# One residual step fewer on node rows: edge rows, a dense first round and a scattered output in a four-layer graph kernel

## The chip, the cores and the metric
One core of one Trainium2 chip runs the whole kernel. The metric is device microseconds of an execution, as the median of the runs shown. One more execution was taken with the hardware profiler; all rows of the trace come from it.

## What is computed
The graph has N = 50000 nodes of width D = 96 and 50000 edges `src -> dst`, sorted by `dst`. Four layers follow each other, each as x = x + layer(relu(layernorm(x))):

```python
x = x + gnn0(h)      # attention with K, Q, V and an edge term, summed per destination
x = x + gnn1(h)      # gated messages from x[src] and 32 edge features, summed, then an MLP and a layernorm
# gnn2: 16 rounds of smoothing over the graph with self loops
h = h0
for _ in range(16):
    h = 0.9 * segment_sum(norm * h[row], col) + 0.1 * h0
x = x + h
# gnn3: one weighted graph convolution with self loops, norm = dinv[row] * ew * dinv[col]
h = relu(layernorm(x))
x = x + segment_sum((h @ W)[row] * norm, col) + b
```

A node that no edge points to has only its self loop: its smoothed value stays its start value, and its last layer needs no neighbour.

## The kernel before
**Layout.** Rows are padded to 128 partitions x 392 columns (`CH`), and one batch is J = 8 columns of all partitions, 1024 rows of 96 floats (384 KB). A pass over nodes or edges has `NB` = 49 batches. Because the edges are sorted by destination, a segment sum is a running sum down the columns of a partition: `scan_step` (L344) issues 16 small VectorE instructions for a batch, and a 128x128 product with `B` carries sums over partition borders at the end of a pass. The sum of a segment stands in the row of the segment's last edge. Segments that begin in an earlier partition are finished in 128 auxiliary rows.

**Gathers.** Whatever a row needs from another row is fetched by `gathers` (L337): eight indirect DMAs for a batch, issued by GpSimd (POOL), each for 128 rows. Stores and plain loads are issued by SyncE (SP).

**Stages.** They run one after the other. Each is a block with its own semaphores, and `retire` (L202) clears these between two stages. I name a stage by the prefix of its tiles:
- n0 (L514): layernorm and the K, V, Q product on nodes; scatters the pointer of each segment into `info_t`.
- e0 (L683): attention on edges, two gathers for a batch (16 issues).
- n1 (L818), e1 (L904): nodes, then edges, of the second layer, one gather for a batch each.
- n2 (L1057): the MLP of the second layer, x2, and the start value y0 of the smoothing, stored to x2_t and to both y tables (L1098).
- r1 (L1255): the first of 16 rounds. From here on the state of a node with in-edges lives in the row of its segment's last edge (tile `H`), so a round is one gather and one scan on edge rows. r1 fetches both y[src] and the start value y[dst], 16 issues for a batch, and stores c_t.
- r (L1354): 15 more rounds in one loop, 8 issues for a batch. A round's first gather waits until all rows of the round before are stored (L1395).
- n3 (L1476): back on node rows: gathers the last round's value, forms x3, layernorm, the product with W, and stores x3_t and z_t.
- e3 (L1594): gathers z[src], weighs and sums it on edge rows, stores agg3_t.
- n4 (L1657): gathers agg3 for each node, forms the output, stores it densely.

**Order.** `skewed` (L111) writes each engine's program as ticks: in tick t each stage function of the engine is run for batch t minus its lag, in the order of the list. K = 4 buffers stand between POOL and the compute engines in the skewed stages; r1, e3, n4 and e0 use two (`batches`, L132, and `ahead`, L143).

Of the kernel before, what the change touches and what calls it, by code (L numbers as in the profile page):

```python
# [17 lines left out]
P = 128  # L18
N = 50000
# [19 lines left out]
VALUES = ROWS  # L39
ROUNDS = 16  # L40
ALPHA = 0.1
NONE = 65535
WZ = D + HEADS
# [67 lines left out]
def skewed(eng, *stages):  # L111


    def tick(q, u):
        for lag, run in stages:
            n, h = q + (u - lag) // K, (u - lag) % K
            if not isinstance(q, int) or 0 <= K * n + h < NB:
                run(K * n + h, n, h)
# [3 lines left out]
    last = (NB - 1 + min(min(lags), 0)) // K  # L122
# [5 lines left out]
    for t in range(last * K, NB + max(lags)):  # L128
        tick(t // K, t % K)
# [28 lines left out]
def program(nc, x, src, dst, edge_attr_32, edge_attr_96, edge_weight,  # L158
# [13 lines left out]
    agg3_t = dram("agg3_t", REG + 1, D)  # L172
# [12 lines left out]
    with outer:  # L185
# [42 lines left out]

        def load_padded(eng, tile, whole, tail, b, done):
# [21 lines left out]
        k_e = sb("k_e", [P, CH])  # L251
        k_z = sb("k_z", [P, 1])
        ptr_n = sb("ptr_n", [P, CH])
        ptr_i = sb("ptr_i", [P, CH], I32)
        yptr_i = sb("yptr_i", [P, CH], I32)
        root = sb("root", [P, CH])
        iroot = sb("iroot", [P, CH])
        dinv = sb("dinv", [P, CH])
# [40 lines left out]
        r_all = sb("r_all", [P, 3, D])  # L299

# [60 lines left out]
        def pointers(own, ptr, no, start, t, to, base):  # L361

            own.do(V.scalar_tensor_tensor(out=t, in0=ptr[:], scalar=-1.0, in1=start[:], op0=ALU.mult, op1=ALU.add))
            own.do(V.tensor_scalar(t, t, -float(base), None, ALU.add))
            own.do(V.tensor_tensor(t, t, no[:], ALU.mult))
            own.do(V.scalar_tensor_tensor(out=t, in0=ptr[:], scalar=float(base), in1=t, op0=ALU.add, op1=ALU.add))
            own.add(V.tensor_copy(to[:], t))


        with ExitStack() as ph:  # L370
# [12 lines left out]
            aux_f = sb("aux_f", [P, 1], F32, ph)  # L383
            tmp = sb("tmp", [P, CH], F32, ph)
# [16 lines left out]
            with nc.Block() as block:  # L401
                @block.sync
                def _(sp):
# [13 lines left out]
                    for t in (agg0_t, agg1_t, agg3_t):  # L417
# [3 lines left out]
                    sp.wait_ge(s_tail, 16 * 12)  # L421
# [4 lines left out]
                def _(pool):  # L426
# [10 lines left out]
                    G.iota(aux_i[:], [[1, 1]], base=AUX, channel_multiplier=1).then_inc(s_iota, 1)  # L437
# [1306 lines left out]
```

## Time and profile before

| | us |
|---|---|
| median of 3 runs | 15979.43 |
| range of the runs | 15961.53 to 15987.55 |
| span of the profiled execution, first to last instruction | 13552.9 |
| time outside the span (median less span) | 2426.5 |
| POOL busy | 9980.6, 74% |
| DVE (VectorE) busy | 6176.6, 46% |
| PE (TensorE) busy | 6161.5, 45% |
| ACT (ScalarE) busy | 3099.7, 23% |

The profiled execution's own time is given as its span alone; what lies around it is known only as the difference to the median. Busy time counts instructions, not the time between the issues of two DMAs. Because the stages follow each other, an average over the span says little: a stage is read by itself, from its first to its last POOL instruction.

### The profile page before, as it was taken

How to read it: one execution, taken by the hardware profiler on the slowest of the kernel's cores; microseconds unless marked ns; L12 is line 12 of the kernel's file. 1: busy time of each engine (PE TensorE's matmuls, PEld its weight loads, DVE VectorE, ACT ScalarE, POOL GpSimd, SP SyncE). 2: the span in 40 equal slices, each digit the busy share in tenths (PEclk: the TensorE clock that was granted, in tenths of full speed). 3: DMA queues.
4: the chain of work that ended last, by engine and by line, in shares of the span. 5: the costliest groups of instructions: out<-in, count | busy, mean ns of one | idle time of the engine just before them, and what ended most of it. 6: DMA issues, size and time to landing. Idle time of an engine off the chain costs nothing. (4 is left out here: it accounts for less than half of the span.)

```text
span 13552.9 us, 124135 instructions
## 1 busy us (share of the span) xinstructions
PE 6161.5 (45%) x16702; PEld 3564.8 (26%) x16702; DVE 6176.6 (46%) x21955; ACT 3099.7 (23%) x11470; POOL 9980.6 (74%) x10210
## 2 busy tenths in 40 slices
PE   6422105873002555555555555555555555544000
PEld 4322103542001322223323332323322322233000
DVE  4344455596343444444444444444444444444533
ACT  5300133394000222222222222222222222233000
POOL 7677777676777777777777777777777777777777
PEclk8655557886555777777777777777777777755555
DMA  5433353374223333333333333333333333344245
GB/s 150 120 99 100 109 145 97 92 216 142 76 75 89 117 112 112 118 112 112 116 112 112 118 112 112 116 112 112 117 112 112 116 113 112 116 132 129 73 116 140
DMA packets 855833, 1558.86 MB, mean 115 GB/s; under 512 B 321698, under 2 KB 378674, under 8 KB 855666
## 3 DMA queue, kind: packets, MB, share of 16 engines
q1 hardware_dynamic: 523217, 1053.28, 22.9%
q0 software_dynamic: 332448, 504.04, 16.3%
q14 instruction: 148, 1.20, 0.0%
q8 instruction: 20, 0.33, 0.0%
HBM read 954.90 MB, written 602.08 MB: 115 GB/s over the span
## 5 line engine op out<-in xcount | busy, mean ns | idle before, releaser
L340 POOL DMA_INDIRECT r_g<-y_t,idx_s x6272 | 6051.0, 965 | 2128.7 <-issue 2115.0
L349 DVE SCALAR_TENSOR_TENSOR r_S<-r_S,scan_s,r_g 128x96 f32<-128x96 f32 x6272 | 2020.3, 322 | 4670.1 <-DMA r_g<-y_t,idx_s 3968.8
L1421 PE MATMUL r_pu<-r_S,ident 128*128 128x384 f32 x2940 | 1883.7, 787 | 3127.9 <-DVE F L351 3127.9
L1443 ACT ACTIVATE H<-r_pu,k_e 128x96 f32 (+1 forms) x5880 | 1443.3, 356 | 6059.3 <-PE r_pu L1421 6059.3
L351 DVE SCALAR_TENSOR_TENSOR F<-r_g,scan_s,F 128x96 f32<-128x96 f32 x6272 | 1967.6, 314 | 0.0
L1421 PEld LDWEIGHTS r_pu<-r_S,ident 128*128 128x128 f32 x2940 | 737.9, 276 | 3947.0 <-DVE F L351 3583.5
L1415 PE MATMUL r_pu<-H,ident 128*128 (+1 forms) x2940 | 1633.0, 646 | 101.5 <-DMA r_c<-c_t 101.5
L340 POOL DMA_INDIRECT n_ag<-agg_t,idx_s x1176 | 1227.2, 1044 | 395.8 <-issue 368.4
L1416 PE MATMUL r_pu<-r_c,ident 128*128 128x384 f32 x2940 | 1441.4, 578 | 0.0
L1415 PEld LDWEIGHTS r_pu<-H,ident 128*128 128x128 f32 x2940 | 824.4, 281 | 816.9 <-issue 683.4
L1416 PEld LDWEIGHTS r_pu<-r_c,ident 128*128 128x128 f32 x2940 | 712.4, 242 | 599.2 <-issue 383.0
L340 POOL DMA_INDIRECT e_g<-z_t,idx_s x392 | 397.2, 1013 | 148.5 <-issue 120.8
L340 POOL DMA_INDIRECT n_y<-y_t,idx_s x392 | 403.0, 1028 | 135.4 <-issue 118.0
L751 PE MATMUL e_eo<-w_e,e_eaT 97*128 97x96 f32 x784 | 182.7, 428 | 676.3 <-ACT e_eaT L772 676.3
L1297 PE MATMUL r_pc<-r_S,B 128*128 128x96 f32 x2 | 0.7, 475 | 1059.9 <-DVE H L1342 1059.9
L556 POOL DMA_INDIRECT info_t<-seg_s,idx_s x392 | 382.1, 975 | 120.2 <-issue 119.2
L1289 POOL DMA_INDIRECT r_c<-y_t,r_dst_s x392 | 378.0, 964 | 119.5 <-issue 119.5
L340 POOL DMA_INDIRECT e_kv<-kv_t,idx_s x392 | 377.9, 964 | 119.4 <-issue 119.4
L340 POOL DMA_INDIRECT e_x<-rec_t,idx_s x392 | 375.4, 958 | 119.4 <-issue 117.0
L731 POOL DMA_INDIRECT e_q<-q_t,dst_s x392 | 371.2, 947 | 119.5 <-issue 114.3
L349 DVE SCALAR_TENSOR_TENSOR e_S<-e_S,scan_s,e_g 128x96 f32<-128x96 f32 (+1 forms) x1176 | 380.3, 323 | 58.0 <-DVE e_g L800 9.4
L351 DVE SCALAR_TENSOR_TENSOR F<-e_g,scan_s,F 128x96 f32<-128x96 f32 (+1 forms) x1176 | 375.6, 319 | 0.0
(233 smaller groups left out, 7251.4 us busy)
## 6 DMA issues: line engine op xcount, KB each, us to landing
y_t<-H SPq DMA_DIRECT2D x784, 384.0 KB, 2.4
r_c<-c_t SPq DMA_DIRECT2D x735, 384.0 KB
r_g<-y_t,idx_s POOLq DMA_INDIRECT x6272
n_x<-x_t SPq DMA_DIRECT2D x147, 384.0 KB, 4.5
kv_t<-n_kvq SPq DMA_DIRECT2D x49, 768.0 KB, 3.7
agg_t<-e_S SPq DMA_DIRECT2D x98, 384.0 KB, 2.6
x_t<-n_x SPq DMA_DIRECT2D x98, 384.0 KB, 2.4
y_t<-n_y SPq DMA_DIRECT2D x98, 384.0 KB
```

The lines of the kernel that those rows point to most:

```text
L340: G.indirect_dma_start(out=to(j), out_offset=None, in_=table, in_offset=bass.IndirectOffsetOnAxis(ap=idx_s[:, h, j:j + 1], axis=0)).then_i ...
L349: own.add(V.scalar_tensor_tensor(out=S[:, h % slots, j, 0:w], in0=before, scalar=scan_s[:, h, j, 0:1], in1=g[:, j, 0:w], op0=ALU.mult, op1 ...
L351: last = V.scalar_tensor_tensor(out=F[:, 0:w], in0=g[:, j, 0:w], scalar=scan_s[:, h, j, 1:2], in1=F[:, 0:w], op0=ALU.mult, op1=ALU.add)
L556: G.indirect_dma_start(out=info_t, out_offset=bass.IndirectOffsetOnAxis(ap=idx_s[:, h, j:j + 1], axis=0), in_=seg_s[:, h, j, :], in_offset ...
L731: G.indirect_dma_start(out=gq[:, h, j, :], out_offset=None, in_=q_t, in_offset=bass.IndirectOffsetOnAxis(ap=dst_s[:, h, j:j + 1], axis=0)) ...
L751: last = T.matmul(eo[g][:, j, :], eaT[:, h, g, j * P:(j + 1) * P], w_e[:], start=True, stop=True)
L1289: G.indirect_dma_start(out=cs[:, h, j, :], out_offset=None, in_=y_t[0][0:ROWS, :], in_offset=bass.IndirectOffsetOnAxis(ap=dst_s[:, h, j:j ...
L1297: T.matmul(pc[:], B[:], S[:, 0, J - 1, :], start=True, stop=True).then_inc(s_cr, 1)
L1415: T.matmul(pu[h % 2][g][:], ident[:], cols(H, b)[:, c, :], start=True, stop=False)
L1416: T.matmul(pu[h % 2][g][:], ident[:], cs[:, h % 2, c, :], start=False, stop=False)
L1421: last = T.matmul(pu[h % 2][g][:], ident[:], S[:, h % 2, 4 * g:4 * g + 4, :], start=False, stop=True)
L1443: last = A.activation(v[:, j, :], pu[h % 2][j // 4][:, j % 4, :], ACT.Copy, scale=k[:, j:j + 1])
```

## The change
- n2 stores one wide table `yx_t` (start value, x2 and five degree factors, 197 floats a row) in place of x2_t. The two y tables are now stored out of the first 96 columns of that tile. ScalarE copies the degree factors into it.
- r1 becomes r0. Its second gather fetches the 788-byte rows of yx_t by `dst` where it fetched 384-byte rows of y; it keeps the degree factors per edge row and stores x2 per edge row too. In the same stage all nodes are treated as if they had no in-edges: dense load of yx_t, x3, layernorm, product with W, output, stores to z_t and to `out`.
- The loop r has 14 rounds where it had 15 (`MID`).
- A new stage l does the last round: after the scan it forms x3, layernorm and the product with W on edge rows, and stores both there. It takes the place of n3.
- e3 gathers z, sums, and finishes the output on edge rows (four more VectorE operations for a batch), and scatters it into `out` with eight indirect DMAs for a batch. Rows that end no segment are skipped by an index out of bounds. n4 and agg3_t are gone.
- In l and e3 a 50th batch (`NX`) handles the auxiliary rows; the tables on edge rows have eight more columns (`CHS`). The pointer arithmetic for y rows is replaced by a pointer that n0 scatters along.

```diff
-VALUES = ROWS
+CHS = CH + J
+SLOTS = P * CHS
+YW = 2 * D + 5
+NX = NB + 1
+OFX = [len(range(h, NX, K)) for h in range(K)]
...
-    x2_t = dram("x2_t", ROWS, D)
-    x3_t = dram("x3_t", ROWS, D)
+    yx_t = dram("yx_t", ROWS, YW)
+    x2s_t = dram("x2s_t", SLOTS, D)
+    x3s_t = dram("x3s_t", SLOTS, D)
     rec_t = dram("rec_t", ROWS, TR)
-    y_t = [dram(f"y{k}_t", VALUES + REG, D) for k in range(2)]
-    c_t = dram("c_t", ROWS, D)
-    z_t = dram("z_t", ROWS, D)
+    y_t = [dram(f"y{k}_t", ROWS + SLOTS, D) for k in range(2)]
+    c_t = dram("c_t", SLOTS, D)
+    z_t = dram("z_t", ROWS + SLOTS, D)
...
-                        after(sp, s_x2, b + 1)
-                        sp.dma_start(rows_of(x2_t, 0, b), x2[:, h]).then_inc(s_st[h], 16)
+                        after(sp, s_kc, b + 1)
                         after(sp, s_y0, b + 1)
+                        sp.dma_start(rows_of(yx_t, 0, b), yx[:, h]).then_inc(s_st[h], 16)
                         for t in y_t:
-                            sp.dma_start(rows_of(t, 0, b), y0[:, h]).then_inc(s_st[h], 16)
+                            sp.dma_start(rows_of(t, 0, b), yx[:, h, :, 0:D]).then_inc(s_st[h], 16)
...
+                        A.copy(yx[:, h, :, 2 * D:YW], cols(kc_n, b)).then_inc(s_kc, 1)
+                        ln_norm(act, b, yx[:, h, :, D:2 * D], yx[:, h, :, 0:D], rn2[:, h], s_sn, ACT.Relu
+                                ).then_inc(s_y0, 1)
...
+                    skewed(sp, (-5, load), (0, store_z), (1, store_c), (2, store_y))
...
+                    def step(b, n, h):
+                        after(pool, s_ix, 2 * b + 2)
+                        after(pool, s_y, b - 3)
+                        pool.wait_ge(s_cx[h], 32 * n)
                         gathers(y_t[0][0:ROWS, :], lambda j: g_[:, h, j, :], h, s_g[h])
                         for j in range(J):
+                            G.indirect_dma_start(out=yx[:, h, j, :], out_offset=None, in_=yx_t,
                                                  in_offset=bass.IndirectOffsetOnAxis(ap=dst_s[:, h, j:j + 1], axis=0)
...
+                    skewed(pe, (0, product), (-1, turn))
...
+                    skewed(act, (-2, slots), (1, keep), (-2, norm), (-1, turned),
+                           (-3, lambda b, n, h: ln_root(act, b, mv[:, h], rn[:, h], s_mv, s_sd)))
...
+                    def begin(b, n, h):
+                        after(dve, s_kc, b + 1)
+                        dve.wait_ge(s_cx[h], 32 * n)
+                        V.tensor_tensor(cs[:, h], yx[:, h, :, 0:D], wide(kc_e, b, 1), ALU.mult).then_inc(s_ck, 1)
+                        after(dve, s_ck, b + 1)
+                        ownb.step(b)
+                        ownb.add(V.tensor_tensor(bt[:, h % 2], cs[:, h], yx[:, h, :, 0:D], ALU.add))
+                        ownb.end()
+                    def value(b, n, h):
+                        own.step(b)
+                        after(dve, s_ms, b + 1)
...
+                        dve.wait_ge(s_st[h], 16 * n)
+                        after(dve, s_b, b + 1)
+                        own.do(V.tensor_tensor(ys[:, h], S[:, h % 2], bt[:, h % 2], ALU.add))
+                        V.tensor_tensor(ys[:, h], ys[:, h], wide(kc_e, b, 0), ALU.mult).then_inc(s_y, 1)
+                    def add(b, n, h):
+                        dve.wait_ge(s_xn[h], 16 * (n + 1))
+                        after(dve, s_h, b - 3)
+                        V.tensor_tensor(x3[:, h], xn[:, h % 2, :, 0:D], xn[:, h % 2, :, D:2 * D], ALU.add
+                                        ).then_inc(s_x3, 1)
+                        after(dve, s_x3, b + 1)
+                        after(dve, s_rn, b - 3)
+                        ln_stats(dve, own1, b, x3[:, h], st[:, h], mv[:, h], s_mv)
...
+                    def finish(b, n, h):
+                        dve.wait_ge(s_sz[h], 16 * n)
+                        for g in range(2):
+                            c = slice(4 * g, 4 * g + 4)
+                            after(dve, s_pz, 2 * b + 1 + g)
+                            V.tensor_copy(zt[:, h, c, :], po[g][:]).then_inc(s_z, 1)
+                        after(dve, s_z, 2 * b + 2)
+                        dve.wait_ge(s_so[h], 48 * n)
+                        own3.step(b)
+                        own3.do(V.tensor_tensor(ot[:, h], zt[:, h], x3[:, h], ALU.add))
+                        own3.end()
+                        V.tensor_tensor(ot[:, h], ot[:, h], r_all[:, 2:3, :].to_broadcast([P, J, D]), ALU.add
+                                        ).then_inc(s_o, 1)
+                    skewed(dve, (-2, scale), (0, finish), (-3, add), (1, begin), (1, value))
+                    finish_round(dve, first, s_cr, 1, zx[:, 0:D], s_zv, pc)
...
+            MID = ROUNDS - 2
...
+                    skewed(sp, (-1, edges_only(load)), (0, edges_only(load_x2)), (2, store_x3), (5, store_z), total=NX)
...
-                        gathers(y_t[1], lambda j: yg[:, h, j, :], h, s_g[h])
+                        after(pool, s_ss, b - 3)
+                        gathers(y_t[0], lambda j: g_[:, h, j, :], h, s_g[h])
                     skewed(pool, (0, step))
...
+                    skewed(pe, (1, edges_only(add)), (0, edges_only(start)), (5, product), (4, turn), total=NX)
...
+                    def value(b, n, h):
+                        after(act, s_up, b + 1)
+                        after(act, s_x3, b - 1)
+                        for j in range(J):
+                            last = A.activation(xv[:, h % 2, j, :], pu[h % 2][j // 4][:, j % 4, :], ACT.Copy,
+                                                scale=cols(kc_e, b)[:, j, 4:5])
+                        last.then_inc(s_xv, 1)
+                    def weigh(b, n, h):
+                        act.wait_ge(s_sz[h], 16 * n)
+                        for j in range(J):
+                            if j % 4 == 0:
+                                after(act, s_pz, 2 * b + 1 + j // 4)
+                            last = A.activation(zt[:, h, j, :], po[j // 4][:, j % 4, :], ACT.Copy,
+                                                scale=cols(kc_e, b)[:, j, 3:4])
+                        last.then_inc(s_z, 1)
+                    skewed(act, (-2, edges_only(slots)), (1, edges_only(value)), (3, norm), (5, weigh), (4, turned),
+                           (2, lambda b, n, h: ln_root(act, b, mv[:, h], rn[:, h], s_mv, s_sd)), total=NX)
...
+                    def sums(b, n, h):
+                        own.step(b)
+                        after(dve, s_ms, b + 1)
+                        after(dve, s_up, b - 1)
+                        s_g.wait(dve, h, 16 * J * (n + 1))
+                        scan_step(dve, own, h, D, g_[:, h], S, 2, s_ss, b + 1)
+                        own.end()
...
+                    skewed(dve, (0, edges_only(sums)), (3, scale), (2, add), total=NX)
...
+                    def scatter(b, n, h):
+                        after(pool, s_io, b + 1)
+                        after(pool, s_o, b + 1)
+                        pool.sem_inc(s_turn_p)
+                        for j in range(1 if isinstance(b, int) and b == NB else J):
+                            G.indirect_dma_start(
+                                out=out, out_offset=bass.IndirectOffsetOnAxis(ap=dst_s[:, h, j:j + 1], axis=0),
+                                in_=ot[:, h, j, :], in_offset=None, bounds_check=bound, oob_is_err=False
+                            ).then_inc(s_d[h], 16)
+                    skewed(pool, (0, edges_only(step)), (2, scatter), total=NX)
+                    for h in range(K):
...
+                            own.do(V.tensor_tensor(g_[:, h], g_[:, h], scan_s[:, h, :, 2:3].to_broadcast([P, J, D]),
+                                                   ALU.mult))
+                            scan_step(dve, own, h, D, g_[:, h], S)
+                            s_d.wait(dve, h, 16 * J * n)
+                            dve.wait_ge(s_ld[h], 32 * (n + 1))
+                            own.do(V.tensor_tensor(ot[:, h], S[:, h % 2], zo[:, h], ALU.add))
+                            c, w = slice(0, J), J
+                        v = ot[:, h, c, :]
+                        own.do(V.tensor_tensor(v, v, cols(kc_e, b)[:, c, 3:4].to_broadcast([P, w, D]), ALU.mult))
+                        own.do(V.tensor_tensor(v, v, x3[:, h, c, :], ALU.add))
+                        V.tensor_tensor(v, v, r_all[:, 2:3, :].to_broadcast([P, w, D]), ALU.add).then_inc(s_o, 1)
+                        if not end:
+                            own.end()
...
-                        gathers(agg3_t, lambda j: ag[:, h, j, :], h, s_g[h])
```

## Rows read from the trace of the kernel before

**Rows 1.** The page: span, and busy time by engine.
```profile
span 13552.9 us, 124135 instructions
PE 6161.5 (45%) x16702; PEld 3564.8 (26%) x16702; DVE 6176.6 (46%) x21955; ACT 3099.7 (23%) x11470; POOL 9980.6 (74%) x10210
```
**Rows 2.** Groups by line, POOL: count | busy us, mean ns | idle before.
```profile
L340 POOL DMA_INDIRECT r_g<-y_t,idx_s x6272 | 6051.0, 965 | 2128.7 <-issue 2115.0 <-ACT scan_s L1437 12.1 <-DVE F L351 1.5
...
L556 POOL DMA_INDIRECT info_t<-seg_s,idx_s x392 | 382.1, 975 | 120.2 <-issue 119.2 <-DVE seg_s L571 1.0
...
L340 POOL DMA_INDIRECT e_kv<-kv_t,idx_s x392 | 377.9, 964 | 119.4 <-issue 119.4
```
**Rows 3.** Timeline of POOL at stage borders: start us, us, instruction [idle before].
```profile
3178.75 0.95 POOL L340 DMA_INDIRECT n_ag<-agg_t,idx_s  x1 [0.31 <-issue]
3233.36 0.95 POOL L1280 DMA_INDIRECT r_zc<-y_t,idx_z  x1 [53.66 <-ACT scan_s L1309]
...
4270.12 0.95 POOL L340 DMA_INDIRECT r_g<-y_t,idx_s  x1 [12.13 <-ACT scan_s L1437]
...
4778.77 0.95 POOL L340 DMA_INDIRECT r_g<-y_t,idx_s  x1 [14.03 <-issue]
...
11927.68 0.95 POOL L340 DMA_INDIRECT n_y<-y_t,idx_s  x1 [16.15 <-ACT idx_s L1557]
...
12473.98 0.95 POOL L340 DMA_INDIRECT e_g<-z_t,idx_s  x1 [24.12 <-ACT scan_s L1631]
...
13008.18 0.95 POOL L340 DMA_INDIRECT n_ag<-agg_t,idx_s  x1 [12.58 <-issue]
...
13541.67 0.95 POOL L340 DMA_INDIRECT n_ag<-agg_t,idx_s  x1 [0.30 <-issue]
```
**Rows 4.** Timeline of DVE and POOL inside one batch of r1.
```profile
3257.38 0.96 DVE L1338 TENSOR_TENSOR r_c<-r_c,r_t 128x768 f32<-128x768 f32 x1
3257.57 1.58 POOL L340 DMA_INDIRECT r_g<-y_t,idx_s  x1 [0.30 <-issue]
...
3706.57 0.34 DVE L349 SCALAR_TENSOR_TENSOR r_S<-r_S,scan_s,r_g 128x96 f32<-128x96 f32 x1 [6.47 <-DMA r_g<-y_t,idx_s]
...
3710.92 0.31 DVE L351 SCALAR_TENSOR_TENSOR F<-r_g,scan_s,F 128x96 f32<-128x96 f32 x1
```
**Rows 5.** Timeline of ACT and DVE: one batch of r, one of n3.
```profile
8002.77 0.27 ACT L1437 COPY scan_s<-scan 128x24 f32 x1
...
8012.36 1.96 ACT L1443 ACTIVATE H<-r_pu,k_e 128x96 f32 x8 [9.31 <-PE r_pu L1421]
...
12208.45 1.38 DVE L306 BATCH_NORM_STATS2 n_st<-n_x 128x6 f32<-128x96 f32 x8
...
12209.98 0.64 DVE L311 BATCH_NORM_AGGREGATE n_mv<-n_st 128x2 f32<-128x6 f32 x8 [0.15 <-DVE n_st L306]
...
12211.50 1.02 DVE L1548 TENSOR_TENSOR n_z<-n_po,dinv 128x384 f32<-128x384 f32 x2
12211.55 2.97 ACT L329 ACTIVATE n_h<-n_x,n_rn 128x96 f32<-128x96 f32 x8 [0.51 <-DVE n_rn L322]
...
12214.43 1.04 ACT L1567 COPY n_hT<-n_tp 96x512 f32<-96x512 f32 x2
```
**Rows 6.** Windows of r, n3, n2 (ten batches): us, busy by engine, PEclk, DMA share, GB/s.
```profile
4275.00:11920.00 7645.00, 4423.50 (x8845) 2282.72 (x8844) 3264.34 (x11816) 1586.53 (x7334) 5640.60 (x5876) 0.78 0.38 113
11920.00:12470.00 550.00, 265.56 (x1180) 241.23 (x1178) 262.20 (x1082) 214.47 (x596) 402.96 (x392) 0.52 0.44 141
...
2886.00:2992.00 106.00, 84.48 (x398) 51.63 (x397) 99.07 (x455) 100.65 (x226) 81.91 (x80) 0.89 0.76 222
```
**Rows 7.** SP's DMA queue in n0 (60 to 520) and n2 (2690 to 3170): packets, MB, share.
```profile
q1 hardware_dynamic: 103530, 71.61, 49.9%
...
q1 hardware_dynamic: 30757, 84.21, 51.0%
```

More of the change, by code:

```diff
@@ L127, in skewed @@
             tick(q, u)
-    for t in range(last * K, NB + max(lags)):
+    for t in range(last * K, total + max(lags)):
         tick(t // K, t % K)
@@ new lines, in program, with wide, first_slots, finish_round @@
+        nodes.close()
+        def wide(t, b, k):
+            return cols(t, b)[:, :, k:k + 1].to_broadcast([P, J, D])
+        def first_slots(table, first):
+            return table[first:first + SLOTS, :].rearrange("(p j) d -> p j d", p=P)[:, CH, :]
+        def finish_round(dve, own, s_cr, count, before, s_z, pc):
+            dve.wait_ge(s_cr, count)
+            own.do(V.tensor_tensor(Z[:, 0:D], F[:, 0:D], pc[:], ALU.add))
+            own.add(V.memset(F[:], 0.0))
+            own.do(V.tensor_tensor(Z[:, 0:D], Z[:, 0:D], before, ALU.add))
+            V.scalar_tensor_tensor(out=zs[:], in0=Z[:, 0:D], scalar=zx[:, 2 * D:2 * D + 1], in1=z0[:], op0=ALU.mult,
+                                   op1=ALU.add).then_inc(s_z, 1)
@@ new lines, in product @@
+                    def product(b, n, h):
+                        for g in range(2):
+                            after(pe, s_tc, 2 * b + 1 + g)
+                            after(pe, s_z, 2 * b - 1 + g)
+                            for j in range(4):
+                                last = T.matmul(po[g][:, j, :], hT[:, h % 2, g, j * P:(j + 1) * P], w_3[:],
+                                                start=True, stop=True)
+                            last.then_inc(s_pz, 1)
+                    skewed(pe, (0, product), (-1, turn))
@@ L1310, in _, with keep @@
-                    batches(act, step)
+                        A.copy(idx_s[:, h, :], cols(src_i, b)).then_inc(s_ix, 1)
+                        s_d.wait(act, h, 16 * J * n)
+                        A.copy(dst_s[:, h, :], cols(dst_i, b)).then_inc(s_ix, 1)
+                        after(act, s_y, b - 3)
+                        A.copy(scan_s[:, h], cols(scan, b)).then_inc(s_ms, 1)
+                    def keep(b, n, h):
+                        s_d.wait(act, h, 16 * J * (n + 1))
+                        A.copy(cols(kc_e, b), yx[:, h, :, 2 * D:YW]).then_inc(s_kc, 1)
@@ L1626, in _, with slots @@
                 @block.scalar
                 def _(act):
-                    def step(n, h):
-                        act.wait_ge(s_s[h], n)
-                        gather_slots(act, n, h, src_i, s_ix, s_g, 16 * J)
-                        A.copy(scan_s[:, h], cols(scan, 2 * n + h)).then_inc(s_ix[h], 1)
-                    batches(act, step)
+                    def slots(b, n, h):
+                        s_g.wait(act, h, 16 * J * n)
+                        A.copy(idx_s[:, h, :], cols(row_e, b)).then_inc(s_ix, 1)
+                        after(act, s_o, b - 3)
+                        A.copy(scan_s[:, h], cols(scan, b)).then_inc(s_ms, 1)
@@ L1634, in _, with out_slots @@
+                    def out_slots(b, n, h):
+                        s_d.wait(act, h, 16 * J * n)
+                        A.copy(dst_s[:, h, :], cols(out_e, b)).then_inc(s_io, 1)
+                    skewed(act, (-2, edges_only(slots)), (1, out_slots), total=NX)
                 @block.vector
                 def _(dve):
-                    own = Own(dve, s_own, 1 + 2 * J - 1)
-                    own.add(V.memset(S[:], 0.0))
-                    own.do(V.memset(F[:], 0.0))
-                    own.loop()
```

653 lines of the change are left out of this document (341 added, 312 removed).

## The prediction, made before the changed kernel ran

> **What bounds the kernel now.** I read the page first: POOL is busy 74% of the span, no other engine half of it [rows 1]. Then the groups by line for POOL: an indirect DMA holds POOL for 0.95 to 0.98 us whether it gathers 384-byte rows, 768-byte rows (e_kv) or scatters (info_t), and 0.30 us passes before the next [rows 2]. So one issue costs 1.25 us when nothing disturbs it, whatever the row size. The code has 26 passes of 392 issues and one more: 10193, and 10193 x 1.25 = 12741 us of the 13552.9 us span. The kernel is a queue of issues; the other 812 us are idle stage borders and lengthened issues. The timeline of POOL at the borders gives each stage its own length (a stage ends where the next starts, less the idle time shown) [rows 3]:
> - r1: 3234.6 to 4258.0, 1023.4 us, 20.89 for a batch of 16 issues (quiet: 20.0).
> - r: 4270.1 to 11911.5, 7641.4 us, 509.4 for a round including 14.0 between rounds; inside a round 10.11 for a batch of 8 (quiet: 10.0).
> - n3: 522.2, 10.66 a batch. e3: 521.6, 10.65. n4: 534.4, 10.91, and 10.3 us after its last issue.
> - Borders: 53.7 (into r1), 12.1, 16.2, 24.1, 12.6.
>
> What lengthens an issue is seen inside r1 [rows 4]: POOL's instruction that starts at 3257.57, within a VectorE operation on 768 elements with two SBUF inputs, takes 1.58 us where 0.95 is usual. Only an issue that starts inside such an operation pays, so the excess per batch is small: 0.11 us with the scan alone (r), 0.65 with the scan and one wide operation (e3), 0.66 with two (n3), 0.89 with the scan and four (r1), 0.91 with four (n4).
>
> **The change, in issues.** Removed: one round, n3, n4 and r1's sixteen, that is 392 x 5. Added: r0's sixteen, l's eight, the scatter's eight in e3, 392 x 4, and one for the auxiliary rows. Left are 9802, 391 fewer: 489 us at 1.25. The rest is what the new stages give back.
>
> **n2.** Its work is changed in three places. (a) ScalarE copies 40 numbers a partition for each batch, 0.2 to 0.3 us (24 numbers take 0.27 [rows 5]). ACT is busy 100.65 of 106 us for ten batches of 10.6 [rows 6], so 0.53 us a batch is free and covers it; without that cover it would be 10 to 15 us. (b) The wide store adds 101 floats to 1024 rows, 414 KB; SP's queue moves 84.21 MB in 51.0% of 480 us on 16 engines, 21.5 bytes per ns and engine [rows 7], so 1.2 us a batch. (c) The two y stores go out in pieces of 384 bytes. n0 does that with q_t, next to other stores, and runs at 19.5 [rows 7]; if q_t alone makes the difference, a 384 KB store costs 0.45 us more, two of them 0.9. The DMA share of 0.76 [rows 6] is 8.1 us of 10.6; with 1.2 and 0.9 it is 10.2, just under the pace. Bounds: nothing, or 1 us a batch (49 us) if a nearly full queue holds the gathers back. I take 15, near nothing, since 10.2 is still below 10.6.
>
> The Trainium skill, "DMA: Bandwidth & Descriptors", section Specifications, says that transfers below 512 bytes make the DMA engine read, modify and write. If that doubled the y stores, n2 would be DMA-bound at 11.6 us and the time 34 us above my forecast. The rate of n0 shows a far smaller surcharge.
>
> **r0 for r1.** 16 issues, 20.0 us quiet; the longer rows change nothing for POOL, as e_kv shows [rows 2]. VectorE now has per batch: the scan 4.7 us [rows 4], seven wide operations of 0.96 (begin 2, value 2, add 1, finish 2), statistics 2.0, two copies out of PSUM about 1.0 [rows 5], 0.4 of scale: 15 us of 20. ACT has norm 2.97, the transposed copies 1.04 and some copies, about 5. Both fit. The dense part runs two to five ticks ahead through its lags and waits for nothing that POOL produces, and POOL waits for value of four batches back, 60 us of cover. SP issues eight transfers a batch where r1 has two, and waits inside them for s_z, s_o, s_ck, s_y in turn; behind it stands only the load five batches ahead. So the stage stays paced by issues. Excess: not below r1's 0.89, since scan and four operations are still there; n3's 0.66 stands for the dense part; together with one more operation up to 1.75, and 2.9 if each of three separate runs of wide operations catches an issue (3 x 0.65 + 0.9). I take 2.0: 22.0 x 49 = 1078. Its first gather comes later than r1's: ACT's list puts the root of batch 0 ahead of the first index copy, so it waits for a load, an add and statistics: about 10 us more. The border behind it grows from 12.1 to 22, since the scan and begin (6.7 us) now stand behind the last landing, and a copy of out_tail.
>
> **Rounds.** 14 x 509.4 = 7132. The first round also loads H, 384 KB a batch beside 38% DMA share [rows 6]: nothing. Border 16.
>
> **l for n3.** Eight issues, POOL waits for sums of four batches back. VectorE: 4.7 + 1.0 + 2.0 + 0.4 = 8.1. ACT: value 1.96, weigh the same, norm 2.97, copies 1.04 [rows 5], root and slots 0.8: 8.7. PE does what it does in r (4423.5 / 735 = 6.0) and in n3 (265.6 / 49 = 5.4) [rows 6]: 11.4 at the clocks of those windows, 0.78 and 0.52. In n2, where PE has 8.4 us of work in 10.6, the clock is 0.89; scaled to it the sum is 5.3 + 3.2 = 8.5. I take POOL's pace with e3's excess, 10.65 x 49 = 522; bounds 10.1 (r's) and 11.4. The border behind l: n2's 53.7 had a lag of six ticks, n3's 24.1 one of four; l has five and one batch more: 42.
>
> **e3 with the output for e3 and n4.** The same issues as the two together, and their wide operations: 10.65 + 10.91 = 21.56 x 49 = 1056; VectorE has 9.5 us of work in it. The scatter waits for a batch finished a whole tick earlier, so the gather of the next batch is never held up. One issue and the tail: 11.6.
>
> **Sum** from r1's first gather to the end: before 10318. After 10 + 1078 + 22 + 7132 + 16 + 522 + 42 + 1056 + 12 = 9890, 428 less; with n2's 15, 413 less. The span goes to 13140. Outside the span lie 2426 us that no row explains; neither stages nor loops can be seen in it, so I carry it over: 15979 - 413 = about 15565. Were it in proportion to the span (x 1.179), the gain would be 487 and the time 15490.
>
> **Rivals.**
> - *Another engine paces a stage.* In l PE at n3's clock: 6.0 x 0.78 / 0.52 + 5.4 = 14.4 us a batch, 184 us more; with n2 at its upper bound 49 - 15 = 34 more: about 15785. For it: PE waits for other engines in every tick, and n3's low clock. Against it: in n2 the same kind of load has 0.89.
> - *VectorE shuts POOL out, slower than before.* If an issue could not run during any VectorE operation with two SBUF inputs, r0 would take 20.0 + 6.7 + 5.0 = 31.7 (475 us over my term), e3 20.0 + 4.8 + 5.0 = 29.8 (404), l 16.0 (262): 16706. It decides from 39% of that, where the 413 and a further 32 are used up. Against it: r1 would need 28.8 and takes 20.89. For it: r0 leaves VectorE only 5 us free, more crowded than any stage shown. The Trainium skill, "SBUF — State Buffer", section "SBUF: two separate sides", calls the port pair of VectorE and GpSimd an exclusive lock taken also by operations with two SBUF inputs; the trace agrees that such a stall exists, and disagrees that it costs the operation's whole time.
> - *The saving is larger.* r0 at 0.89, e3 at one scan's 0.65, l at 10.1, no surcharge in n2: 140 us less, with the proportional outside 15979 - 553 x 1.179, about 15330.
> - *The change doesn't do what it says,* because idle borders or a serial first stage eat the 489 us: about 15980.
>
> **How the numbers follow.** Forecast 80%; another engine 10%; larger saving 5%; lock-out 3%; nothing 2%. The terms' bounds are, below: r0 -54, e3 -45, l -26, n2 -15, borders -28; above: r0 +43, l +37, n2 +34, borders +12. Half of the proportional outside's 74 goes below. That gives 15400 to 15700, which leaves out most of the 10% above and 5% below. A measurement tells about 0.2%, 32 us, from no change. Faster 0.93 (the first three, less some), same 0.02, slower 0.05.
>
> **What would show it.** POOL's issues: 9802. r0 near 22.0 us a batch and l near 10.7, with POOL idle before issues at 0.30; a wait of POOL on s_y or s_ss would prove another pace. e3 near 21.6. n2 still 10.6 a batch with DMA share near 0.95. Borders of 64, 22, 16, 42 us. Wrong would be a stage whose POOL idle time grows, a mean issue above 1.15 us in r0, or a time outside the span that moved.

## The result, and the profile after

On the chip of the first comparison the changed kernel took 15560.61 us (median of 4 runs, 15546.08 to 15589.12) and the kernel before 15983.49 (median of 4, 15961.53 to 16002.94): a ratio of 0.9737, 95% interval 0.9723 to 0.9751, or 423 us less. The forecast was 15565.

The page of the changed kernel's profiled execution, to be read beside [rows 1], and POOL's groups by line, beside [rows 2] (count | busy us, mean ns | idle before, with what ended it):

```profile
span 15555.2 us, 127954 instructions
PE 6190.4 (40%) x17902; PEld 3704.8 (24%) x17902; DVE 6357.5 (41%) x22965; ACT 3386.6 (22%) x12470; POOL 9532.1 (61%) x9820
```

```profile
L352 POOL DMA_INDIRECT r_g<-y_t,idx_s x5880 | 5634.2, 958 | 3590.5 <-issue 1924.0 <-ACT scan_s L1575 1452.6 <-DVE r_y L1443 177.9
...
L1830 POOL DMA_INDIRECT out<-e_o,e_out_s x393 | 417.7, 1063 | 174.8 <-issue 174.5 <-DVE e_o L1885 0.3
L1353 POOL DMA_INDIRECT r_yx<-yx_t,r_dst_s x392 | 402.0, 1025 | 119.4 <-issue 118.5 <-DVE r_y L1443 0.6 <-DMA x2s_t<-r_yx 0.3
```

POOL does what was forecast: 449 us less busy than in [rows 1], the same mean issue, a scatter of output rows at 1063 ns and a gather of 788-byte rows at 1025. But the span is 2000 us longer than that of the kernel before, and this execution took 15557.04 us, only 1.8 us more than its span. The 2426 us that the prediction carried "outside the span" are inside it. They are gaps, and they repeat. POOL at the borders of r and inside a round (start, us, instruction [idle before <- what ended it]):

```profile
5207.78 0.94 POOL L352 DMA_INDIRECT r_g<-y_t,idx_s  x1 [22.59 <-ACT scan_s L1575]
...
8016.19 0.94 POOL L352 DMA_INDIRECT r_g<-y_t,idx_s  x1 [6.10 <-ACT scan_s L1575]
...
8052.86 0.99 POOL L352 DMA_INDIRECT r_g<-y_t,idx_s  x1 [6.88 <-ACT scan_s L1575]
...
13723.83 0.94 POOL L352 DMA_INDIRECT l_g<-y_t,idx_s  x1 [22.36 <-ACT idx_s L1721]
```

Between the two middle rows lie 24 issues (29.8 us) and one gap, 36.7 us in all, and so it goes on through all rounds. A round takes 607 us here ((13723.83 - 22.36 - 5207.78) / 14) where [rows 3] gave 509.4. Whether the kernel, the change or the chip makes these gaps can't be told from this profile: it was the first question for the experiments.

### The profile page after: what moved, and what is told of

It reads as the page before. It is cut to its first block and busy times, and to the rows that moved or that the text cites. A ratio compares the mean times of both kernels' runs of the same rounds, so it can differ in the third digit from the quotient of the medians.

```text
span 15555.2 us, 127954 instructions
## 1 busy us (share of the span) xinstructions
PE 6190.4 (40%) x17902; PEld 3704.8 (24%) x17902; DVE 6357.5 (41%) x22965; ACT 3386.6 (22%) x12470; POOL 9532.1 (61%) x9820
## 5 line engine op out<-in xcount | busy, mean ns | idle before, releaser
L352 POOL DMA_INDIRECT r_g<-y_t,idx_s x5880 | 5634.2, 958 | 3590.5 <-issue 1924.0
L361 DVE SCALAR_TENSOR_TENSOR r_S<-r_S,scan_s,r_g 128x96 f32<-128x96 f32 x5880 | 1884.9, 321 | 5521.0 <-remote 3601.6
L1581 ACT ACTIVATE H<-r_pu,kc_e 128x96 f32 (+1 forms) x5488 | 1350.5, 368 | 7020.0 <-remote 4524.4
L1559 PE MATMUL r_pu<-r_S,ident 128*128 128x384 f32 x2744 | 1111.1, 531 | 650.6 <-remote 265.9
L352 POOL DMA_INDIRECT n_ag<-agg_t,idx_s x784 | 780.4, 995 | 457.3 <-issue 236.8
L1559 PEld LDWEIGHTS r_pu<-r_S,ident 128*128 128x128 f32 x2744 | 586.5, 217 | 1133.1 <-issue 374.3
L352 POOL DMA_INDIRECT l_g<-y_t,idx_s x392 | 386.4, 986 | 288.5 <-ACT idx_s L1721 120.4
L1373 PE MATMUL d_po<-w,d_hT 96*128 96x96 f32 x784 | 186.7, 430 | 932.6 <-ACT d_hT L1404 532.3
L1830 POOL DMA_INDIRECT out<-e_o,e_out_s x393 | 417.7, 1063 | 174.8 <-issue 174.5
L1353 POOL DMA_INDIRECT r_yx<-yx_t,r_dst_s x392 | 402.0, 1025 | 119.4 <-issue 118.5
```

Source lines behind the costliest of these rows:

```text
L352: G.indirect_dma_start(out=to(j), out_offset=None, in_=table, in_offset=bass.IndirectOffsetOnAxis(ap=idx_s[:, h, j:j + 1], axis=0)).then_i ...
L361: own.add(V.scalar_tensor_tensor(out=S[:, h % slots, j, 0:w], in0=before, scalar=scan_s[:, h, j, 0:1], in1=g[:, j, 0:w], op0=ALU.mult, op1 ...
L1353: G.indirect_dma_start(out=yx[:, h, j, :], out_offset=None, in_=yx_t, in_offset=bass.IndirectOffsetOnAxis(ap=dst_s[:, h, j:j + 1], axis=0) ...
L1373: last = T.matmul(po[g][:, j, :], hT[:, h % 2, g, j * P:(j + 1) * P], w_3[:], start=True, stop=True)
L1559: last = T.matmul(pu[h % 2][g][:], ident[:], S[:, h % 2, 4 * g:4 * g + 4, :], start=False, stop=True)
L1581: last = A.activation(v[:, j, :], pu[h % 2][j // 4][:, j % 4, :], ACT.Copy, scale=k[:, j, 0:1])
```

## The experiments

The kernels of one group ran on one chip, beside the kernel before. The four groups had four chips, none twice; A stands for the first comparison, whose chip may be one of them. Each kernel of group B, and its kernel before, was timed once, the others four times or more. There are two kinds of chips, and that answers the first question: neither the kernel nor the change makes the gaps, but the chip, or the hour at which it was used.

| chip | kernels | kernel before, us | spans |
|---|---|---|---|
| A | first comparison | 15983 | 15555 (after) |
| B | before_again, two_rounds_less | 13479 | 13470, 12034 |
| C | after_again, scatter_eighth, wide_doubled, dense_idle | 13507 | 13078, 12655, 13172, 13048 |
| D | after_third, wide_psum, e3_products_act, products_act | 15955 | 15511, 15589, 15523, 15561 |
| E | products_again, psum_again | 15976 | 15552, 15622 |

Every profiled execution took 1.7 to 1.8 us more than its span. B and C show none of the regular gaps; the span of 13552.9 in [rows 1], whose trace has none either, is of that kind, and the timed runs beside it were of the other.

### The kernel before, and the changed one with two rounds less (chip B)

before_again is the kernel before. two_rounds_less leaves out two of the fourteen steps of r, so its output is that of fewer steps:

```diff
-            MID = ROUNDS - 2
+            MID = ROUNDS - 4
```

> The kernel before, unchanged, for a trace taken like that of after. The span of after (15555.2 us) is as long as its time, while the trace of before spanned 13552.9 us of about 15980. Theory A: the 2426 us are pauses spread over all stages, which the first trace of before did not catch; then this span is near 15980, a round takes about 590 us in place of 509, and DVE and ACT show waits put down to 'remote' every 30 to 40 us. Theory B: the time lies before or behind the span; then the span is near 13553 again and a round is 509 us.

> The changed kernel with 12 rounds in its loop in place of 14 (two smoothing rounds are left out, so the output is not the reference's). It prices a round as timed. If a round costs what the first trace showed, 509 us, the time is 15560 - 1019 = 14541 us. If the pauses come with the rounds' time, each round costs about 604 us (its share of 15555 / 13140) and the time is about 14350 us.

Measured: 13471.72 us with a span of 13470.0, and 12035.92 with 12034.1. Both expectations missed, each for the same reason: they took the 2426 us for a part of every run. The span and the round that theory B gave for before_again come close (13553 and 509, measured 13470 and 507.0), but nothing lies around the span. Neither "gaps in all stages" nor "gaps outside" holds on this chip; there are none. The rounds do tell the price of a round, from the first gather of r to the first of l:

```profile
4302.95 0.94 POOL L352 DMA_INDIRECT r_g<-y_t,idx_s  x1 [20.31 <-ACT scan_s L1575]
...
10401.58 0.94 POOL L352 DMA_INDIRECT l_g<-y_t,idx_s  x1 [16.09 <-ACT idx_s L1721]
```

(10401.58 - 16.09 - 4302.95) / 12 = 506.9 us, as in before_again, whose own borders are these ((11869.46 - 16.16 - 4249.01) / 15 = 507.0):

```profile
3219.18 0.94 POOL L1281 DMA_INDIRECT r_zc<-y_t,idx_z  x1 [58.03 <-ACT scan_s L1310]
...
4249.01 0.94 POOL L341 DMA_INDIRECT r_g<-y_t,idx_s  x1 [12.13 <-ACT scan_s L1438]
...
11869.46 0.94 POOL L341 DMA_INDIRECT n_y<-y_t,idx_s  x1 [16.16 <-ACT idx_s L1558]
...
12407.72 0.94 POOL L341 DMA_INDIRECT e_g<-z_t,idx_s  x1 [25.93 <-ACT scan_s L1632]
...
12925.29 0.94 POOL L341 DMA_INDIRECT n_ag<-agg_t,idx_s  x1 [12.58 <-issue]
```

Two more at that price make 12036 + 1014 = 13050 for the changed kernel, 429 under before.

### The changed kernel on a chip without gaps (chip C)

> The changed kernel itself with one comment line on top, beside the kernel before on the same chip. Theory A (the saving is made of issues and borders, and the time that the timed runs of the first comparison had beyond the 13552.9 us span is idle time spread over stages that both kernels feel about alike): the difference is 421 us wherever it runs; if the kernel before takes about 13478 here, this one takes about 13055, ratio 0.969; if the kernel before takes about 15980, about 15560, ratio 0.974. Theory B (that time is in proportion to the work): the ratio is the same on every chip, 0.974, so 13478 would become 13120.

Measured: 13087.22 us (13079.51 to 13091.04), before 13507.19; ratio 0.9691 (0.9675 to 0.9707), 420 us less. Theory A holds, with two of its numbers met, and B's 0.974 lies outside the interval. The saving is an amount of time, not a share; on D it was 432 us (15954.98 less 15523.36). Its stages, POOL at the borders, beside [rows 3]:

```profile
3238.27 0.94 POOL L1345 DMA_INDIRECT zx<-yx_t,idx_z  x1 [70.08 <-ACT idx_z L1383]
3249.07 1.09 POOL L353 DMA_INDIRECT r_g<-y_t,idx_s  x1 [9.87 <-ACT r_dst_s L1389]
...
4319.40 0.95 POOL L353 DMA_INDIRECT r_g<-y_t,idx_s  x1 [20.44 <-ACT scan_s L1576]
...
11451.00 0.95 POOL L353 DMA_INDIRECT l_g<-y_t,idx_s  x1 [17.04 <-ACT idx_s L1722]
...
12005.29 0.94 POOL L353 DMA_INDIRECT e_g<-z_t,idx_s  x1 [55.69 <-ACT idx_s L1848]
...
13067.58 0.97 POOL L1831 DMA_INDIRECT out<-e_o,e_out_s  x1 [0.30 <-issue]
```

and windows of r0, e3, l, and ten batches of n2 (length, busy by engine, PEclk, DMA share, GB/s), then n2 and n3 of before_again:

```profile
3249.10:4299.00 1049.90, 263.60 (x1176) 240.30 (x1176) 685.56 (x2068) 228.57 (x729) 811.11 (x784) 0.52 0.61 182
12005.30:13068.60 1063.30, 0.74 (x2) 0.50 (x2) 456.18 (x1036) 26.13 (x140) 824.27 (x785) 0.50 0.23 67
...
11460.00:11940.00 480.00, 354.24 (x1582) 236.24 (x1580) 357.99 (x1605) 348.52 (x1271) 365.03 (x378) 0.91 0.67 220
2876.00:2982.00 106.00, 90.21 (x398) 57.57 (x397) 98.78 (x447) 101.15 (x238) 81.29 (x82) 0.81 0.90 256
```

```profile
2876.00:2982.00 106.00, 86.73 (x378) 52.69 (x378) 99.06 (x458) 100.89 (x230) 81.70 (x80) 0.84 0.77 220
11880.00:12370.00 490.00, 246.43 (x1088) 224.12 (x1088) 248.63 (x1030) 201.21 (x558) 375.81 (x375) 0.52 0.48 148
```

### An eighth of the scatters (chip C)

```diff
-                        for j in range(1 if isinstance(b, int) and b == NB else J):
+                        for j in range(1):
```

with the waits on s_d counting 16 for a batch instead of 16 * J.

> e3 scatters only the first of the eight column groups of each batch, so most rows of the output that have in-edges stay as r0 left them; 343 indirect DMAs are gone and nothing else. Theory A (POOL's issues pace e3): against the changed kernel -430 (343 x 1.25) to -470 us (343 x 1.38, the mean that a scatter's issue and the pause behind it take in e3). Theory B (VectorE's chain and the waits between engines pace e3 at about 17 us a batch once the scatters are few): at most -240 us.

Measured: 12656.59 us, 430.6 under after_again: 1.255 us for each of the 343 issues by the medians, and 417 of it in the length of e3 itself. Theory A, at its lower end: an issue taken away saves its quiet price, and the lengthening stays. The window of e3 shows it, 646.1 us for 442 issues, POOL busy 1.134 us an issue where 785 issues had 1.050:

```profile
12003.30:12649.40 646.10, 0.74 (x2) 0.50 (x2) 453.67 (x1036) 26.20 (x139) 501.35 (x442) 0.50 0.33 93
```

### The dense half taken out of r0 (chip C)

```diff
-                    skewed(dve, (-2, scale), (0, finish), (-3, add), (1, begin), (1, value))
+                    skewed(dve, (1, begin), (1, value))
```

and likewise in the lists of ACT, PE and SP.

> r0 without the arithmetic of the dense half: no load of yx_t by rows, no addition, statistics, norm, transposition, product or finish; SP still stores z_t and the output from tiles set to zero once, so z_t and the output rows of nodes without in-edges are zero. It prices what the dense half costs beside the issues. Theory A (the forecast's terms): against the changed kernel -65 us, from 49 x (22.0 - 20.89) for lengthened issues and 10 for the late first gather. Theory A' (the stage's own length of 21.4 us a batch): -36 us, 26 for lengthened issues and 10 for the first gather. Theory B (VectorE's two-input operations shut POOL out for their whole time): -475 us.

Measured: 13040.79 us, 46 under after_again. The window of r0, and its first issues:

```profile
3239.60:4251.30 1011.70, 0.00 (x0) 0.00 (x0) 399.90 (x972) 31.26 (x183) 772.90 (x784) 0.50 0.51 152
```

```profile
3238.36 0.94 POOL L1344 DMA_INDIRECT zx<-yx_t,idx_z  x1 [68.92 <-ACT idx_s L1385]
3239.61 0.95 POOL L352 DMA_INDIRECT r_g<-y_t,idx_s  x1 [0.31 <-issue]
```

So the dense half costs 38.2 us in r0 (1049.9 - 1011.7), all of it POOL's busy time (811.1 - 772.9), and 9.6 at its start: 48 us, between the two estimates. Of the 286 us of VectorE's work that are gone, 139 belong to the three wide operations with two SBUF inputs (47.3, 46.9 and 44.6 us in r0 of after_again). A lock-out for their whole time would have given at least those 139 back; 38 were gained, so it is ruled out in r0. Its recorded -475 was too much for this kernel, which keeps four of the seven wide operations and the scan. POOL's busy time in e3, whose code is the same, moved too, from 824 to 841: that is how far phase alone moves a stage.

### Four more wide operations in e3, from SBUF and from PSUM (chips C, D, E)

```diff
-                    own, first = Own(dve, s_own, 2 * J + 4), Own(dve, s_v)
+                    own, first = Own(dve, s_own, 2 * J + 8), Own(dve, s_v)
...
+                            for _ in range(4):
+                                own.do(V.tensor_tensor(more[:], zo[:, h], x3[:, h], ALU.add))
```

In wide_psum and psum_again the second input is pq, 96 numbers in PSUM, in place of x3.

> e3 with four more VectorE additions of 768 elements a batch, both inputs in SBUF, written to a tile that nobody reads; each takes about 0.96 us, so VectorE is busy 3.8 us a batch longer and still less than the 21.8 us a batch. Theory A (only an issue that starts inside such an operation is lengthened): 0 to +45 us (49 x 0.91). Theory B (POOL issues nothing during such an operation): +188 us (49 x 4 x 0.96).

> e3 with four more VectorE additions of 768 elements a batch, as in the kernel with both inputs in SBUF, which took 71 us more by the medians and 92 us by the stage's length, but with the second input in PSUM (96 numbers, read again for each column group). Theory A (what lengthens POOL's issues is an operation that reads two tiles in SBUF): 0 to +10 us. Theory B (any long VectorE operation beside an issue lengthens it): +71 to +92 us, as before.

> The kernel with four more wide operations a batch in e3 whose second input is in PSUM, once more. Theory A (only two inputs in SBUF lengthen an issue): POOL's busy time in e3 within 17 us of the changed kernel's 824.3, which is how far the same stage moved between kernels that share its code, and the time within 20 us of the changed kernel's (ratio 0.968 to 0.971 if the kernel before takes about 13500). Theory B (any long VectorE operation): 916 us busy and 71 to 92 us more, ratio 0.974 to 0.976.

Measured from SBUF: 13158.52 us, 71 over after_again by the medians, and e3 1155.4 us in place of 1063.3, 92 more, all of it POOL's busy time (916.3 for 824.3). Neither theory: twice my upper bound, half of the lock-out. The timeline of VectorE and POOL shows how it comes about:

```profile
12499.41 0.96 DVE L1882 TENSOR_TENSOR e_more<-e_z,e_x 128x768 f32<-128x768 f32 x1
12500.40 0.96 DVE L1883 TENSOR_TENSOR e_o<-e_S,e_z 128x768 f32<-128x768 f32 x1
12501.53 0.96 DVE L1886 TENSOR_TENSOR e_o<-e_o,kc_e 128x768 f32<-128x768 f32 x1 [0.17 <-DVE e_o L1883]
```

```profile
12498.54 1.68 POOL L1831 DMA_INDIRECT out<-e_o,e_out_s  x1 [0.31 <-issue]
12500.52 1.68 POOL L1831 DMA_INDIRECT out<-e_o,e_out_s  x1 [0.30 <-issue]
12502.51 0.98 POOL L352 DMA_INDIRECT e_g<-z_t,idx_s  x1 [0.30 <-issue]
```

While wide operations follow each other without a gap, an issue takes 1.68 us and the next comes 1.98 us after it, the length of two operations, instead of 1.25. A run of such operations pays again and again; in [rows 4] I had seen one issue caught and taken that for the price of a run.

From PSUM POOL's busy time in e3 is 811.0 (chip D) and 803.9 (E), against 812.0 of the changed kernel beside it on D: no lengthening at all by operations just as long (954 ns). (803.9 lies 20 us under the 824.3 of psum_again's expectation, away from theory B's 916.) The issues themselves show it without a comparison of chips. In wide_psum 133 issues start inside one of the added operations and take 965 ns in the mean (127 in psum_again, 964); in wide_doubled 98 issues do, and take 1621. VectorE and POOL of wide_psum:

```profile
14931.74 3.92 DVE L1884 TENSOR_TENSOR e_more<-e_z,e_pq 128x768 f32<-128x768 f32 x4 [0.22 <-DVE F L363]
```

```profile
14932.20 0.97 POOL L1832 DMA_INDIRECT out<-e_o,e_out_s  x1 [0.30 <-issue]
14933.48 0.97 POOL L1832 DMA_INDIRECT out<-e_o,e_out_s  x1 [0.30 <-issue]
```

It isn't the reading of the same 96 numbers again that spares them: the kernel's own addition of r_all reads 96 numbers again too, from SBUF, and the 40 issues that start inside it in after_again take 1555 ns.

In time the kernels with PSUM were not free, and both were measured only on chips with gaps. On D wide_psum took 15562.5 us against 15523.4, with ratios to before of 0.9749 (0.9726 to 0.9771) and 0.9730 (0.9713 to 0.9748), which overlap, and e3 18 us longer. On E psum_again took 15611.27 us, ratio 0.9763 (0.9748 to 0.9778), 46 us more than products_again beside it; its e3 took 1135.5 us, 32 more than after_third's. That is outside the 20 us of theory A, and the ratio alone would have fitted theory B; POOL's busy time doesn't. POOL waits there for finished batches, up to 13 us at a time, 93 us on E after its first gather where the changed kernel on D has 54:

```profile
15248.99 1.00 POOL L1833 DMA_INDIRECT out<-e_o,e_out_s  x1 [13.01 <-issue]
```

Such differences lie in part in stages whose code is unchanged: l took from 652 to 681 us in the seven traces with gaps, so less than about 30 us isn't resolved there.

So theory A is right on the issues, wrong on the time where there are gaps, and its time on a chip without gaps stays unmeasured. The Trainium skill, "SBUF — State Buffer", section "SBUF: two separate sides", has VectorE hold the port pair that it shares with GpSimd for the whole of an operation with two SBUF inputs, against a GpSimd operation that reads SBUF, and GpSimd wait. The issues above agree that two SBUF inputs are what counts; but POOL loses half of the added operations' time (92 of 188 us), not all. That the rest of an issue goes on beside them is an inference; the trace shows an issue only as a whole.

### Products moved to ScalarE (chips D, E)

```diff
-                            own.do(V.tensor_tensor(g_[:, h], g_[:, h], scan_s[:, h, :, 2:3].to_broadcast([P, J, D]),
-                                                   ALU.mult))
...
+                        for j in range(J):
+                            last = A.activation(g_[:, h, j, :], g_[:, h, j, :], ACT.Copy, scale=scan_s[:, h, j, 2:3])
+                        last.then_inc(s_mk, 1)
```

and the same for the product with kc_e; products_act and products_again do it also for the two products of r0.

> The same result with two of e3's five wide VectorE operations (the products with the mask and with the node's factor) as eight ScalarE operations of 96 elements each. Theory A (each wide operation with two inputs in SBUF costs POOL 0.36 to 0.47 us, from the kernel with four more: 71/196 and 92/196): -35 to -46 us against the changed kernel. Theory B (the longer chain ScalarE - VectorE - ScalarE - VectorE makes POOL wait for finished batches): 0 or slower, with POOL idle before the scatters in e3.

> The same, and in r0 also two of seven: the products of yx with the two factors go to ScalarE. Theory A: a further -24 (the dense half's three wide operations cost 36 us in all, so 0.25 each a batch) to -46 us (0.47 each), in all -60 to -92 us. Theory B (ScalarE, 4.9 us a batch busy in r0 now and 8.8 then, or VectorE waiting for it, holds POOL up in r0): r0 no shorter than 21.4 us a batch, so no more than the kernel with e3 alone.

> The kernel with two products of r0 and two of e3 on ScalarE, once more. In its first run POOL's busy time was 792.7 us in e3 against 812.0 of the changed kernel beside it, and 807.7 against 802.9 in r0. Theory A (each wide two-input operation fewer saves POOL about 0.4 us wherever it is): e3 20 to 46 us and r0 24 to 46 us under the 1063.3 and 1049.9 us of the changed kernel, ratio to the kernel before 0.962 to 0.966 if that takes about 13500. Theory B (what counts is which operation an issue happens to meet, and that is fixed by when the gathers land): e3 about 20 us shorter, r0 unchanged or longer, ratio 0.967 to 0.969.

Measured on D: 15525.02 and 15556.47 us against 15523.36 of after_third, whose own expectation was

> The changed kernel once more, as the ground for the other three of this group. If the kernel before takes about 13500 here, 13085 and e3 21.7 us a batch; if it takes about 15980 (the condition of the first comparison), 15560, and then e3 is lengthened least of the stages that gather, since its batches are 20 us long and it has four buffers.

and on E 15564.9, ratio 0.974 (0.9727 to 0.9753). No gain. The windows of e3 (POOL's busy time) of after_third, then of e3_products_act:

```profile
14399.10:15502.90 1103.80, 811.97 (x785) 0.50 0.23 64
```

```profile
14411.00:15513.80 1102.80, 791.73 (x785) 0.50 0.23 64
```

Issues are 20 us shorter in all, less than theory A's 35 to 46, and POOL waits as much longer for finished batches: with ScalarE in the chain twice, theory B's waits take the gain. In r0 the issues are no shorter (802.9 us before, 808.2 and 805.9 after), and the border behind it grows from 22.5 to 36 and 60 us. A likely cause is that the lists of ScalarE and VectorE now hand each batch over twice and the last batches run one after the other; no run separates it, and with r0 unchanged the same border is 22.5 to 29.8 us. All of this was seen only on chips with gaps. The row of products_again:

```profile
5214.29 0.95 POOL L353 DMA_INDIRECT r_g<-y_t,idx_s  x1 [60.04 <-ACT scan_s L1585]
```

### What the gaps are

Windows of after_third in a round, around the end of one wait of VectorE:

```profile
8024.00:8027.00 3.00, 0.00 (x0) 0.00 (x0) 0.00 (x0) 0.00 (x0) 1.78 (x2) 1.00 0.23 47
8027.00:8030.00 3.00, 0.00 (x0) 0.00 (x0) 0.00 (x0) 0.00 (x0) 0.00 (x0) 0.73 0.01 2
8030.00:8033.00 3.00, 0.00 (x0) 0.00 (x0) 2.65 (x10) 2.78 (x14) 0.00 (x0) 0.50 0.00 0
8033.00:8036.00 3.00, 0.00 (x0) 0.00 (x0) 2.34 (x10) 1.45 (x8) 2.12 (x3) 0.50 0.88 285
```

The wait, 18 us, is put down to no instruction of this core, and ScalarE (ACT) ends one of 21.5 us in the same moment:

```profile
8030.21 0.32 DVE L362 SCALAR_TENSOR_TENSOR r_S<-r_S,scan_s,r_g 128x96 f32<-128x96 f32 x1 [17.95 <-remote]
8030.22 1.96 ACT L1582 ACTIVATE H<-r_pu,kc_e 128x96 f32 x8 [21.54 <-remote]
```

POOL issues until its four buffers are full, and from 8027 to 8033 the DMA engines move nothing (share 0.01 and 0.00), while VectorE scans a whole batch: its data had landed. It isn't the landings that come late either. Those that the trace has for this batch's gathers end at 8017.4 (not every landing is recorded), and ScalarE's step waits for no gather at all. What both wait for is s_up, the sign that PE has added a batch to r_pu. PE's operation for it ends at 8010.2 (the end is modelled), and PE has begun its next one at 8017.1:

```profile
8008.71 1.45 PE L1560 MATMUL r_pu<-r_S,ident 128*128 128x384 f32 x4
8017.11 1.64 PE L1554 MATMUL r_pu<-H,ident 128*128 x2 [6.95 <-issue]
```

The trace records the sign at 8030.07, 19.9 us after the operation; in the three other periods between 7970 and 8103 it is 19.9, 18.5 and 20.1 us. In after_again it comes 0.01 us after. All 170 waits of VectorE over 10 us that are put down to "remote" between 5300 and 13000 us of after_third, all of them in rounds, end with s_up. In the same stretches SP is slow. From the store of y_t to the load of r_c it takes 7.03 us here and 0.46 us in after_again:

```profile
8008.99 0.70 SPq L1518 DMA_DIRECT2D y_t<-H  x1
8016.02 0.70 SPq L1513 DMA_DIRECT2D r_c<-c_t  x1
```

```profile
7965.22 0.35 SPq L1518 DMA_DIRECT2D y_t<-H  x1
7965.68 0.36 SPq L1513 DMA_DIRECT2D r_c<-c_t  x1
```

Its register and semaphore instructions, 0.03 us in the median, take over 0.4 us, mostly 0.70, in 1892 of 8616 cases; in each trace with gaps it is 1787 to 1900 of them, in each without gaps two. So the gaps are delays in the handing over between engines, of PE's sign and in SP's queue, and not in the moving of data. Whether one causes the other, and what causes both, the trace doesn't show; no run here can, since the same kernels ran with and without them.

after_third's expectation that e3 suffers least is met: it goes from 21.7 to 22.5 us a batch, l with its batches of ten from 10.2 to 13.3. The reason that it gave is not: r0 has batches of 20 us and four buffers too, and goes from 21.4 to 24.8. e3 differs in having no product of PE in its batches, which fits the late sign but wasn't tried.

## Why the prediction was right, and where it was lucky

The time (15565 for 15560.61) and the saving (forecast 413, measured 423 on A, 420 on C) are both right; term by term it is less even. Forecast changes against the changes from before_again (B) to after_again (C), in us:

| term | forecast | measured |
|---|---|---|
| n2 | +15 | -2 (both on B: 511.7, 513.6) |
| border into r0, first gather | +10 | +22 |
| r0 for r1 | +55 (22.0 a batch) | +33 (21.43) |
| border r0, r | +10 | +8 |
| one round less | -509 | -507; C itself is 1.3 a round slower, +18 |
| l for n3 | 0 (10.65) | -14 (10.18) |
| border l, e3 | +18 (42) | +30 (55.7) |
| e3 for e3 and n4, border | -13 (21.56) | +11 (21.70) |
| tail | +1 | -1 |

The sum of the right column is -402, and -420 without the 18 of chip C. The two spans differ by 392: the other 10 us lie in stages ahead of n2, where chip C is slower too (its kernel before takes 28 us more than B's).

- **Issues.** Right. 391 fewer, and an issue is worth 1.255 us when taken away (scatter_eighth). Row size plays no part: the median issue of r_yx is 949 ns, that of e_kv 949.
- **n2.** The cover held: DMA share 0.90 where I expected 0.95, and 10.4 us a batch by the stage's length (10.5 in before_again), ACT 101.2 us busy of 106. The stores cost nothing that can be seen.
- **r0.** Over-sized by 28 us. The dense half costs 0.78 us a batch, and the measured 21.43 is near the middle between r1's 0.89 of excess and my 2.0. The guess of three runs of operations each catching an issue was too many.
- **l.** Not bound by PE: its clock is 0.91, near n2's 0.89 [rows 6], not 0.52 as in n3, and PE has 354 us in 480. The rival that took n3's clock is out. Its excess is that of r, not of e3, which I had taken; but e3 itself, with its one wide operation, has 10.31 a batch in before_again and 10.65 in [rows 3], so it was a value that moves. 23 us too much.
- **Borders.** Under-sized by 12 at r0 (9.9 for the late first gather was right; n2's own tail is 70.1 us instead of 58.0) and by 14 at e3 (55.7 for 42; that it has five lags and a batch more, each a full pass through ACT, PE and VectorE, is the likely reason). Neither was priced by a run.
- **e3.** Right as a sum of rows, 1063.3 for 1056. The mechanism behind my excess was too weak, as wide_doubled shows, but the rows that I added carried its full effect.
- **Outside the span.** Wrong as a reading. Nothing lies outside; span and median came from executions of two kinds. Carrying the 2426 over unchanged gave the right sum because the saved stages and the new ones meet about the same gaps. They need not have: a round is 98 us longer on A than on C (607, 508), r0 170 us, l 154, e3 41. So one round less saves 98 us more where there are gaps, and other stages must give that back; which do can't be shown stage by stage, since no profile of the kernel before has gaps. I had put half of a "proportional" 74 us into the range; the measured savings on A and C differ by 3, on D and C by 12.
- **Lock-out.** Ruled out at its full price by dense_idle (38 us for 139 of two-input operations) and wide_doubled (92 for 188).

No kernel of these that computes the whole result beats the changed one.

## What to carry to other kernels

Where one engine's queue of issues bounds the kernel, count issues, and then price borders by the lags and depth of the stage that drains: both were under-sized here, by 26 us together, about as much as r0 (28) and l (23) were over-sized. Before a median is compared with a span, see whether they come from executions of one kind. Shorter issues are worth nothing where the chain behind them gets longer: a product moved to an idle engine adds two handovers to each batch, and on the chips with gaps, where handovers are slow, it gained nothing. When a trace names no releaser for a wait, look which engines wake in the same moment and what they have in common.

## What the hardware showed that was not expected

- The same kernel takes 13479 and 13507 us on two chips, and 15955 to 15983 on two others and in the first comparison. In the latter VectorE and ScalarE wait 16 to 18 and 20 to 22 us once in 36.6 us for a sign of PE that is recorded 18.5 to 20.1 us late, while SP's control instructions take 0.70 us instead of 0.03, and POOL stands still for 6 to 7 us of each period in a round.
- An issue of an indirect DMA beside back-to-back VectorE operations with two SBUF inputs takes 1.68 us instead of 0.95; beside operations as long with one input in PSUM it isn't lengthened (965 ns in the mean of 133).
- Stores of 384-byte rows at a DMA share of 0.90 cost n2 nothing.
